# Wide attention on one Trainium2 core: the output projection moved behind the next fills, four exponentials moved ahead of the contexts' copy

## The chip, the cores and the metric

The kernel runs on one core of one Trainium2 chip. The time is device microseconds (us) for one execution of the whole program. Before the change three executions took 1840.51 to 1841.86 us, with a median of 1841.23 us. The core's engines are PE (TensorE; its weight loads are listed as PEld), ACT (ScalarE), DVE (VectorE), POOL (GpSimd) and SP, which issues the loads. Each engine runs its own instructions in order and waits on semaphores for the others.

## The reference

The program is a stack of four gated layers on `x` of shape (32, 128, 128); each has a cross-attention on `ctx` and a feed-forward part. Only the second cross-attention (layer 1, "wide") is touched by the change:

```python
x = x + tanh(g_xattn[1]) * xattn(layernorm(x), ctx, ctx, w_q, w_k, w_v, w_o)
# 32 batches, 128 queries, 128 keys, 16 heads of 64
# q = x w_q^T, k = ctx w_k^T, v = ctx w_v^T       (128 -> 1024 each)
# probs = softmax(q k^T / 8), causal over the 128 x 128 pairs
# out = (probs v) w_o^T                           (1024 -> 128)
```

All of it is in float32; only the causal mask is added in bfloat16.

## The kernel before

The wide attention is the function `attention_wide`. Its unit is a step `n` of 0 to 63: one batch and half of its heads (8 of 16). Every engine has its own loop over `n`, unrolled in the program, and the order of the calls in it is the order on the engine; nothing reorders them. In its iteration `n` PE works on three steps at once: it computes the scores of `n+1`, transposes the probabilities of `n`, and multiplies the contexts of `n-1` with the values.

- `score(n)` writes the causal mask (L1862, four bfloat16 matmuls of 512 columns) and then the products of queries and keys (L1867) into one of two score tiles of two banks each.
- DVE takes the row maxima (`maximum`, L2014). ACT makes the eight exponentials, four per call of `exponents(n, h)`, h = 0 and 1 (L1956). DVE inverts the row sums of each four (`invert`, L2022), POOL multiplies (L1819).
- `turn(n)` (L1907) transposes the probabilities on PE; it waits for both halves from POOL. DVE copies the result back (`copy_turned`, L2007).
- `contexts(n)` (L1883) writes the tile `heads`, a single bank. ACT copies it to `heads_t` (`context_copy`, L1947). `project_out(n)` (L1895) multiplies `heads_t` with `w_o` into `y_ps`. After the second half of a batch DVE adds `y_ps` to `x` (L2028) and takes the statistics (L2033).

Queries, keys and values come in groups of two batches, that is, of four steps. A group has 13 **fills**: x (the normalised input transposed, L1839), k0 to k3 and q0 to q3 (L1848), v0 to v3 (L1842). Each is written by PE (`make`) into one of two banks, `made0` and `made1` in turn, and copied to SBUF by ACT (x, q; L1935, L1938) or DVE (k, v; L2000) in `keep`. So a fill may start only when the fill **two before it** has been copied: `await_kept(pe, f - 2)`. Fills are made one group ahead of their use, at fixed places of the loop (`quarter`): two ahead of `score`, the rest behind `contexts`.

I name the stretches of PE from one mask to the next by what lies in them, in the order in which they follow each other: stretch **Q** (behind its contexts the fill q1, then, for the next iteration, q2 and q3), stretch **V** (v0; v1, v2), stretch **X** (v3; x, k0) and stretch **K** (k1, k2; k3, q0). The semicolon is the border of two iterations; `project_out` stands on it in the kernel before.

```python
                await_kept(pe, f - 2)
                pe.wait_ge(s["heads_done"], n + 1)      # project_out
                wait(act, s["acc_done"], n - 1)         # context_copy
```

Of the kernel before, what the change touches and what calls it, by code (L numbers as in the profile page):

```python
# [24 lines left out]
def wait(eng, sem, value):  # L25

    if isinstance(value, int) and value <= 0:
        return
    eng.wait_ge(sem, value)
# [1712 lines left out]
def attention_wide(nc, st, arg):  # L1742

    layer, PAIR, OCT = 1, 2 * DKW, 2
    NO, CH = NB * OCT, 4
    with ExitStack() as ctx:
# [39 lines left out]
        def place_of(group, kind, part):  # L1786
            return group * NF + order.index((kind, part))

        def fills(n):

            group, part = divmod(n + 4, 4)
            return [group * NF + i for i in quarter[part]] if group < NGR else []

        def await_kept(eng, f):
            if f >= 0:
                own, count = kept_count(f)
                eng.wait_ge(s[own + "_kept"], count)

        def real(n):
            return 0 <= n < NO  # L1800

        def rows(h):
            return slice(h * DKW, (h + 1) * DKW)
# [19 lines left out]
        def _(pe):  # L1823
            pe.wait_ge(st.loads["wide"].sem, st.loads["wide"].total)

            def make(f):
                group, place = divmod(f, NF)
                kind, part = order[place]
                r, out = group % 2, made[f % 2]
                if kind == "x":  # L1830
                    pe.wait_ge(s["xn_done"], group + 1)
                elif (kind, part) == ("k", 0):
                    pe.wait_ge(ctx_in[r], 16 * (group // 2 + 1))
                elif (kind, part) == ("q", 0):
                    await_kept(pe, place_of(group, "x", 0))
                await_kept(pe, f - 2)
                if kind == "x":
                    for u in range(2):
                        last = nc.tensor.transpose(out[:, u * S:(u + 1) * S], xn[:, r, u * D:(u + 1) * D], st.ident[:, :])  # L1839
                elif kind == "v":  # L1840
                    b, half = divmod(part, 2)
                    last = nc.tensor.matmul(out[:, :], ctx_t[:, r, b * S:(b + 1) * S], w_v[:, half * 512:half * 512 + 512],  # L1842
                                            start=True, stop=True)
                else:
                    w, moving = (w_k, ctx_t) if kind == "k" else (w_q, xn_t)
                    for c in range(2):
                        first = (2 * part + c) * PAIR
                        last = nc.tensor.matmul(out[:, c * 2 * S:(c + 1) * 2 * S], w[:, first:first + PAIR], moving[:, r, :],  # L1848
                                                start=True, stop=True)
                last.then_inc(s["made_done"], 1)  # L1850

            def score(n):
                if not real(n):
                    return
                b, o = divmod(n, OCT)
                group, u = divmod(b, 2)
                await_kept(pe, place_of(group, "k", 3))
                await_kept(pe, place_of(group, "q", 3))
                wait(pe, s["pt_done"], 2 * n - 2)
                for h, table in enumerate((st.causal, st.causal_swapped)):  # L1860
                    for r in range(2):
                        nc.tensor.matmul(scores[n % 2][rows((r + h) % 2), h * 512:h * 512 + 512], st.identb[rows(r), rows(r)],  # L1862
                                         table[rows(r), :].unsqueeze(1).to_broadcast([DKW, CH, S]), start=True, stop=False,
                                         skip_group_check=True)
                for c in range(CH):
                    for h in range(2):
                        last = nc.tensor.matmul(scores[n % 2][:, h * 512 + c * S:h * 512 + (c + 1) * S],  # L1867
                                                q_t[rows(h), group % 2, CH * o + c, u * S:(u + 1) * S],
                                                k_t[rows(h), group % 2, CH * o + c, u * S:(u + 1) * S],
                                                start=False, stop=(c == CH - 1), skip_group_check=True)  # L1870
                last.then_inc(s["s_done"], 1)
# [15 lines left out]
            def project_out(n):  # L1887
                if not real(n):
                    return
                b, o = divmod(n, OCT)  # L1890
                pe.wait_ge(s["heads_done"], n + 1)
                if o == 0:
                    wait(pe, s["x_done"], b)
                for c in range(CH):
                    last = nc.tensor.matmul(y_ps[:, 0:D], heads_t[:, n % 2, c * S:(c + 1) * S], w_o[:, CH * o + c, :],  # L1895
                                            start=(o == 0 and c == 0), stop=(o == OCT - 1 and c == CH - 1))
                last.then_inc(s["acc_done"], 1)

            def turn(n):
                if not real(n):  # L1900
                    return
                pe.wait_ge(s["prob_done"], 2 * n + 2)
                for h in range(2):
                    for c in range(CH):
                        for r in range(2):
                            at = r * 512 + (CH * h + c) * DKW
                            last = nc.tensor.transpose(scores[n % 2][:, at:at + DKW], probs[rows(r), n % 2, h, c * S:(c + 1) * S],  # L1907
                                                       st.ident[rows(r), rows(r)])
                last.then_inc(s["t_done"], 2)

            for n in range(-4, NO + 1):
                todo = fills(n)
                for f in todo[:2]:
                    make(f)
                score(n + 1)
                turn(n)
                contexts(n - 1)
                for f in todo[2:]:
                    make(f)
                project_out(n - 1)  # L1920

        @block.scalar
        def _(act):
            ln_scalar(act)

            def keep(f):
                group, place = divmod(f, NF)
                kind, part = order[place]
                if kept_by[place] != "act":
                    return  # L1930
                act.wait_ge(s["made_done"], f + 1)
                if kind == "x":
                    if group >= 2:
                        act.wait_ge(s["made_done"], place_of(group - 2, "q", 3) + 1)
                    last = nc.scalar.activation(xn_t[:, group % 2, :], made[f % 2][:, 0:2 * S], ACT.Copy)  # L1935
                else:
                    wait(act, s["s_done"], 4 * (group - 1))
                    last = nc.scalar.activation(q_t[:, group % 2, 2 * part:2 * part + 2, :].rearrange("p c q -> p (c q)"),  # L1938
                                                made[f % 2][:, :], ACT.Copy, scale=scale)
                last.then_inc(s["act_kept"], 1)  # L1940

            def context_copy(n):
                if not real(n):
                    return
                act.wait_ge(s["pv_done"], n + 1)
                wait(act, s["acc_done"], n - 1)
                nc.scalar.activation(heads_t[:, n % 2, :], heads[:, :], ACT.Copy).then_inc(s["heads_done"], 1)  # L1947

            def exponents(n, h):
                if not real(n):  # L1950
                    return
                act.wait_ge(s["max_done"], n + 1)
                wait(act, s["t_done"], 2 * (n - 2) + h + 1)
                for c in range(CH):
                    i = CH * h + c
                    last = nc.scalar.activation(probs[:, n % 2, h, c * S:(c + 1) * S],  # L1956
                                                scores[n % 2][:, i * S:(i + 1) * S], ACT.Exp,
                                                bias=neg_max[:, n % 2, i:i + 1], accum_out=row_sum[:, n % 2, i:i + 1])
                last.then_inc(s["exp_done"], 1)

            for n in range(-4, NO + 1):
                todo = fills(n)
                for f in todo[:2]:
                    keep(f)
                context_copy(n - 1)
                exponents(n + 1, 0)
                for f in todo[2:]:
                    keep(f)
                exponents(n + 1, 1)
# [308 lines left out]
```

## Time and profile before

| | us |
|---|---|
| median of three executions | 1841.23 |
| profiled execution, its own time | 1840.51 |
| its span | 1838.7 |
| wide attention, from the first mask on PE to the last statistics on DVE | 347.3 to 799 |
| of it one group of four steps, in the steady part | 27.72 |

The span is what the profiler saw from the first to the last instruction; 1.8 us of the execution lie around it. The page lists PE as busy for 92% of the span. In the wide attention every engine's busy time in a group is the same from one group to the next, so one group stands for all of the steady part. In the timeline a fill of queries or keys is four instructions (two matmuls, each in two float32 passes), a fill of values two, a projection eight. A matmul's listed duration holds the time until its result has landed, so that durations overlap; what a piece of work costs PE is read from start to start.

### The profile page before, as it was taken

How to read it: one execution, taken by the hardware profiler on the slowest of the kernel's cores; microseconds unless marked ns; L12 is line 12 of the kernel's file. 1: busy time of each engine (PE TensorE's matmuls, PEld its weight loads, DVE VectorE, ACT ScalarE, POOL GpSimd, SP SyncE). 2: the span in 40 equal slices, each digit the busy share in tenths (PEclk: the TensorE clock that was granted, in tenths of full speed). 3: DMA queues.
4: the chain of work that ended last, by engine and by line, in shares of the span. 5: the costliest groups of instructions: out<-in, count | busy, mean ns of one | idle time of the engine just before them, and what ended most of it. 6: DMA issues, size and time to landing. Idle time of an engine off the chain costs nothing. (4 is left out here: it accounts for less than half of the span.)

```text
span 1838.7 us, 46448 instructions
## 1 busy us (share of the span) xinstructions
PE 1693.0 (92%) x17680; PEld 1105.1 (60%) x17680; DVE 1084.1 (59%) x2348; ACT 870.4 (47%) x2175; POOL 639.9 (35%) x1103
## 2 busy tenths in 40 slices
PE   5999959799999999867988999979999989999798
PEld 2555544577777777665775555546777755555454
DVE  5677657566666666545166676653233236777576
ACT  3555426455655655533544444434343436544354
POOL 4467508322323223300021555510000004676673
PEclk9999959899999999957999999989999989999899
DMA  4000041000000000010101000000000010000000
GB/s 114 2 2 3 2 117 35 9 7 5 8 7 5 7 7 5 2 46 6 41 0 53 2 3 3 3 2 1 1 0 0 0 35 13 2 3 3 1 24 24
DMA packets 47822, 27.64 MB, mean 15 GB/s; under 512 B 11024, under 2 KB 44560, under 8 KB 47632
## 3 DMA queue, kind: packets, MB, share of 16 engines
q1 hardware_dynamic: 42896, 24.64, 4.8%
q8 instruction: 133, 2.18, 0.5%
q10 hardware_dynamic: 4736, 0.35, 0.2%
q14 instruction: 57, 0.47, 0.1%
HBM read 22.88 MB, written 2.10 MB: 14 GB/s over the span
## 5 line engine op out<-in xcount | busy, mean ns | idle before, releaser
L771 DVE TENSOR_REDUCE neg_max<-scores 128x8 f32<-128x1024 f32 x192 | 235.0, 1224 | 134.7 <-PE scores L560 48.9
L1819 POOL TENSOR_TENSOR probs<-probs,inverse 128x512 f32<-128x512 f32 x128 | 133.2, 1041 | 324.6 <-DVE inverse L2022 324.5
L528 PE MATMUL scores<-k_diag,q_all 32*128 32x512 f32 x768 | 216.0, 639 | 0.9 <-DVE dropped L2158 0.9
L542 PE MATMUL turned<-q_diag,k_all 32*128 32x512 f32 x768 | 216.4, 638 | 0.0
L706 ACT ACTIVATE probs<-turned 128x1024 f32<-128x1024 f32 x128 | 131.1, 1024 | 176.5 <-PE turned L574 176.5
L412 POOL TENSOR_TENSOR k_diag<-k_all,hmask 128x512 f32<-128x512 f32 x96 | 100.0, 1043 | 324.2 <-ACT k_all L681 288.4
L1956 ACT ACTIVATE probs<-scores,neg_max 128x128 f32<-128x128 f32 x512 | 180.7, 387 | 5.3 <-DVE neg_max L2014 5.3
L1478 ACT ACTIVATE hidden_f<-hb_f,b_f 128x512 f32<-128x512 f32 x128 | 87.9, 687 | 128.7 <-PE hb_f L1425 128.4
L1434 PEld LDWEIGHTS yb_f<-w_f,hidden_f 128*128 128x128 f32 x1024 | 119.2, 192 | 14.8 <-issue 14.8
L1947 ACT ACTIVATE heads_t<-heads 128x512 f32<-128x512 f32 x64 | 38.2, 597 | 174.5 <-PE heads L1883 174.5
L1434 PE MATMUL yb_f<-w_f,hidden_f 128*128 128x128 f32 x1024 | 119.3, 275 | 0.0
L1956 ACT ACTIVATION_READ_ACCUMULATOR probs<-scores,neg_max 128x1 f32 x512 | 116.7, 228 | 0.0
L1425 PE MATMUL hb_f<-xn_all_f,w_f 128*128 (+1 forms) x256 | 116.5, 599 | 0.0
L1503 DVE TENSOR_TENSOR y_sum_f<-yb_f,b_f 128x512 f32<-128x512 f32 x32 | 22.1, 692 | 150.2 <-PE yb_f L1434 150.2
L418 POOL TENSOR_TENSOR q_diag<-q_all,hmask 128x512 f32<-128x512 f32 x96 | 100.0, 1041 | 30.3 <-PE turned L574 21.3
L608 PEld LDWEIGHTS heads<-probs,ones_pad 128*32 128x32 f32 x3072 | 78.0, 109 | 46.9 <-issue 46.5
L706 ACT ACTIVATE probs<-turned,key_cols 128x1024 f32<-128x1024 f32 x64 | 71.4, 1115 | 70.7 <-PE turned L574 70.7
L597 PE MATMUL heads<-probs,v_pad 128*32 128x128 f32 x3072 | 103.8, 276 | 0.3 <-ACT probs L706 0.2
L608 PE MATMUL heads<-probs,ones_pad 128*32 128x128 f32 x3072 | 103.8, 276 | 0.0
L778 DVE RECIPROCAL inverse<-heads 128x128 f32<-128x128 f32 x96 | 91.0, 948 | 13.8 <-PE heads L608 7.3
L2014 DVE TENSOR_REDUCE neg_max<-scores 128x8 f32<-128x1024 f32 x64 | 78.2, 1222 | 35.3 <-PE scores L1867 35.3
L597 PEld LDWEIGHTS heads<-probs,v_pad 128*32 128x32 f32 x3072 | 78.0, 109 | 33.9 <-issue 31.6
(305 smaller groups left out, 3628.3 us busy)
## 6 DMA issues: line engine op xcount, KB each, us to landing
ctx_t<-in_ctx_t_dram SPq DMA_DIRECT2D x24, 256.0 KB, 2.9
w_f<-in_L_ffn_W_dram SPq DMA_DIRECT2D x16, 256.0 KB, 3.1
x_state<-in_x_dram SPq DMA_DIRECT2D x4, 512.0 KB, 7.6
ctx_t<-in_ctx_t_dram SPq DMA_DIRECT2D x16, 128.0 KB, 2.1
out_dram<-x_state SPq DMA_DIRECT2D x7, 256.0 KB, 2.3
w_f<-in_L_ffn_We_dram SPq DMA_DIRECT2D x1, 1024.0 KB, 7.1
taps_f<-in_L_ffn_conv_w_dram SPq DMA_DIRECT2D x1, 768.0 KB, 6.4
w_e_f<-_ffn_expert_weights_dram SPq DMA_DIRECT2D x1, 512.0 KB, 4.3
```

The source lines that it names most:

```text
L412: p.tensor_tensor(k_diag[:, b % 2, :, :], cols(k_all, b, S).unsqueeze(1).to_broadcast([P, 4, S]), st.hmask4[:, :].unsqueeze(2).to_broadcas ...
L418: p.tensor_tensor(q_diag[:, b % 2, :, :], cols(q_all, b, S).unsqueeze(1).to_broadcast([P, 4, S]), st.hmask4[:, :].unsqueeze(2).to_broadcas ...
L528: last = nc.tensor.matmul(scores[pair][:, (g % 2) * 512:(g % 2 + 1) * 512], cols(q_all, b, S)[quad_rows(g), :], k_diag[quad_rows(g), b % 2 ...
L542: nc.tensor.matmul(turned[:, (g % 2) * 512:(g % 2 + 1) * 512], cols(k_all, b, S)[quad_rows(g), :], q_diag[quad_rows(g), b % 2, :, :].rearr ...
L597: nc.tensor.matmul(heads[b % 2][32 * j:32 * j + 32, 0:S], v_pad[:, b % 2, 128 * g + 32 * j:128 * g + 32 * j + 32], probs[:, b % 2, g // 2, ...
L608: last = nc.tensor.matmul(heads[b % 2][32 * j:32 * j + 32, S:2 * S], ones_pad[:, (3 - g) * DK:(3 - g) * DK + 32], probs[:, b % 2, g // 2, ...
L706: nc.scalar.activation(probs[:, b % 2, pair, :], turned[:, :], ACT.Exp, **bias).then_inc(s["exp_done"], 1)
L771: v.tensor_reduce(neg_max[:, b % 2, 8 * pair:8 * pair + 8], scores[pair][:, :].rearrange("p (h k) -> p h k", k=S), axis=X_AXIS, op=ALU.max ...
L1425: nc.tensor.matmul(hb[c][:, :], w1[:, e, c * P:(c + 1) * P], cols(xn_all, k, BT), start=True, stop=True).then_inc(h_done, 1)
L1434: last = nc.tensor.matmul(yb[e % 2][:, j * D:(j + 1) * D], hidden[:, e % 2, c, j * S:(j + 1) * S], w2[:, e, c, :], start=(c == 0), stop=(c ...
L1819: nc.gpsimd.tensor_tensor(p4, p4, inverse[:, n % 2, CH * h:CH * h + CH].unsqueeze(2).to_broadcast([P, CH, S]), ALU.mult).then_inc(s["prob_ ...
L1956: last = nc.scalar.activation(probs[:, n % 2, h, c * S:(c + 1) * S], scores[n % 2][:, i * S:(i + 1) * S], ACT.Exp, bias=neg_max[:, n % 2, ...
```

## The change

In PE's loop `project_out` goes from the end of the iteration, behind the fills `todo[2:]`, to the place between the fills `todo[:2]` and `score` of the next iteration. In ACT's loop `exponents(n + 1, 0)` goes ahead of `context_copy(n - 1)`. Nothing is computed otherwise, and the number of instructions of every engine is the same.

```diff
-            for n in range(-4, NO + 1):
+            for n in range(-4, NO + 2):
                 todo = fills(n)
                 for f in todo[:2]:
                     make(f)
+                project_out(n - 2)
                 score(n + 1)
                 turn(n)
                 contexts(n - 1)
                 for f in todo[2:]:
                     make(f)
-                project_out(n - 1)
...
                 for f in todo[:2]:
                     keep(f)
+                exponents(n + 1, 0)
                 context_copy(n - 1)
-                exponents(n + 1, 0)
                 for f in todo[2:]:
                     keep(f)
                 exponents(n + 1, 1)
```

PE, stretch X of the kernel before, from the contexts (`heads`) to the next mask (`causal`); `made_1` is the two banks of layer 1, first with v3, then with x and k0:

```order
L1883 MATMUL heads<-probs_t,v_sb 64x128 x8
L1842 MATMUL made_1<-w_v,ctx_t 128x512
L1895 MATMUL y_ps<-w_o,heads_t 128x128 x4
L1839 MATMUL made_1<-ident,xn 128x128 x2
L1848 MATMUL made_1<-ctx_t,w_k 128x256 x2
L1862 MATMUL scores_1<-causal,identb 64x512 x2
```

The same place of the changed kernel:

```order
L1883 MATMUL heads<-probs_t,v_sb 64x128 x8
L1842 MATMUL made_1<-w_v,ctx_t 128x512
L1839 MATMUL made_1<-ident,xn 128x128 x2
L1848 MATMUL made_1<-ctx_t,w_k 128x256 x2
L1895 MATMUL y_ps<-w_o,heads_t 128x128 x4
L1862 MATMUL scores_1<-causal,identb 64x512 x2
```

The projection no longer stands between v3 and the fills x and k0; the three fills follow each other without a break. The same holds for the other three stretches.

ACT beside the stretches K and Q of the kernel before; the first copy to `q_t` is q0, the one between the exponentials q1, the last two q2 and q3:

```order
L1938 ACTIVATE q_t<-made_1 128x512
L1947 ACTIVATE heads_t<-heads 128x512
L1956 ACTIVATE probs,row_sum<-scores_1,neg_max 128x128 x4
L1938 ACTIVATE q_t<-made_1 128x512
L1956 ACTIVATE probs,row_sum<-scores_1,neg_max 128x128 x4
L1938 ACTIVATE q_t<-made_1 128x512 x2
```

The same place of the changed kernel, from the four exponentials on:

```order
L1956 ACTIVATE probs,row_sum<-scores_1,neg_max 128x128 x4
L1947 ACTIVATE heads_t<-heads 128x512
L1938 ACTIVATE q_t<-made_1 128x512
L1956 ACTIVATE probs,row_sum<-scores_1,neg_max 128x128 x4
L1938 ACTIVATE q_t<-made_1 128x512 x2
```

The copy of the contexts now stands between the first four exponentials and q1's copy; q1's copy still has the copy of the contexts and four exponentials ahead of it.

## Rows read from the trace of the kernel before

**Rows 1.** The page: busy time by engine; granted clock of TensorE in 40 slices.

```profile
PE 1693.0 (92%) x17680; PEld 1105.1 (60%) x17680; DVE 1084.1 (59%) x2348; ACT 870.4 (47%) x2175; POOL 639.9 (35%) x1103
...
PEclk9999959899999999957999999989999989999899
```

**Rows 2.** Busy time by stretch, one group: length, engines, granted clock, DMA share, GB/s.

```profile
386.75:414.47 27.72, 27.20 (x283) 20.97 (x282) 17.70 (x36) 15.92 (x73) 8.33 (x8) 1.00 0.02 7
```

**Rows 3.** Waits in 559.77:587.49: total us, times, longest us.

```profile
PEld scores L1907 <- POOL probs L1819: 0.9, 2, 0.5
PE scores L1907 <- POOL probs L1819: 0.5, 2, 0.4
```

**Rows 4.** Timeline of PE, same group: start, us, instruction, [idle before <-releaser].

```profile
559.77 0.40 PE L1862 MATMUL scores<-causal,identb 64*64 64x512 bf16 x2
...
569.72 1.13 PE L1842 MATMUL made<-w_v,ctx_t 128*128 128x512 f32 x2
570.68 1.05 PE L1895 MATMUL y_ps<-w_o,heads_t 128*128 128x128 f32 x8
...
574.62 0.71 PE L1907 MATMUL scores<-ident,probs 64*128 64x64 f32 x16 [0.35 <-POOL probs L1819]
...
576.29 1.99 PE L1848 MATMUL made<-ctx_t,w_k 128*128 128x256 f32 x8
578.12 1.05 PE L1895 MATMUL y_ps<-w_o,heads_t 128*128 128x128 f32 x8
...
583.78 1.13 PE L1848 MATMUL made<-xn_t,w_q 128*128 128x256 f32 x4
...
587.49 0.40 PE L1862 MATMUL scores<-causal,identb 64*64 64x512 bf16 x2
```

**Rows 5.** Timeline, same group: DVE's copy of k1; DVE, ACT and PEld in stretch Q.

```profile
577.46 0.69 DVE L2000 COPY k_t<-made 128x512 f32<-128x512 f32 x1 [0.73 <-PE made L1848]
...
582.38 1.23 DVE L2014 TENSOR_REDUCE neg_max<-scores 128x8 f32<-128x1024 f32 x1 [0.96 <-PE scores L1867]
...
583.89 0.60 ACT L1947 ACTIVATE heads_t<-heads 128x512 f32<-128x512 f32 x1 [2.36 <-PE heads L1883]
584.39 0.36 ACT L1956 ACTIVATE probs<-scores,neg_max 128x128 f32<-128x128 f32 x1
...
585.76 0.62 ACT L1938 ACTIVATE q_t<-made 128x512 f32<-128x512 f32 x1
...
586.43 0.73 PEld L1848 LDWEIGHTS made<-xn_t,w_q 128*128 128x128 f32 x4 [0.17 <-ACT q_t L1938]
```

**Rows 6.** Timeline of the stage's start: fills v3, x, k0, with no projection yet.

```profile
348.74 1.12 PE L1842 MATMUL made<-w_v,ctx_t 128*128 128x512 f32 x2
...
349.71 0.38 PE L1839 MATMUL made<-ident,xn 128*128 128x128 f32 x2
...
350.00 0.68 DVE L2000 COPY v_sb<-made 128x512 f32<-128x512 f32 x1
...
350.80 0.73 PEld L1848 LDWEIGHTS made<-ctx_t,w_k 128*128 128x128 f32 x4 [0.95 <-issue]
...
350.83 1.10 PE L1848 MATMUL made<-ctx_t,w_k 128*128 128x256 f32 x4 [0.74 <-DVE v_sb L2000]
```

**Rows 7.** Timeline of the stage's end, PE, where no fills are left.

```profile
775.30 0.71 PE L1907 MATMUL scores<-ident,probs 64*128 64x64 f32 x16 [1.54 <-POOL probs L1819]
...
777.73 1.16 PE L1895 MATMUL y_ps<-w_o,heads_t 128*128 128x128 f32 x8 [0.70 <-ACT heads_t L1947]
778.82 0.40 PE L1862 MATMUL scores<-causal,identb 64*64 64x512 bf16 x2
...
779.16 1.16 PE L1867 MATMUL scores<-k_t,q_t 64*128 64x128 f32 x16
...
788.42 0.71 PE L1907 MATMUL scores<-ident,probs 64*128 64x64 f32 x16 [2.97 <-POOL probs L1819]
```

**Rows 8.** Busy time by stretch, the stage's last 12 us; columns as in rows 2.

```profile
788.00:800.00 12.00, 8.41 (x64) 7.03 (x64) 2.15 (x5) 1.45 (x3) 0.63 (x9) 0.56 0.00 0
```

## Prediction

> **What bounds the kernel now.** I read the page first: PE is listed as busy for 92% of the span, twice as long as ACT [rows 1], so a change that touches only the order in one stage has to be read from that stage's PE. The busy time by stretch comes next: in one group of the wide attention PE is busy for 27.20 of 27.72 us at a granted clock of 1.00, DVE for 17.70, ACT for 15.92, POOL for 8.33 [rows 2]. The stage is bound by PE's sequence, and what the change can give is what PE waits for. The waits of one group name only one thing of size: PE's transposes wait for POOL's probabilities twice in a group, 0.5 us in PE's own account and 0.9 us in that of its weight loads, which start first [rows 3]; one of the two is seen in the timeline in stretch K [rows 4].
>
> The wait of the projection for ACT's copy of the contexts is not worth anything. From v3 to the projection it is 0.96 us where one fill stands between contexts and projection, and from k1 to the projection 1.83 us where there are two [rows 4]. The second fill is thus 0.87 us; the first has 0.1 us more, which I take for the change from the contexts' half-width weights, as it is there in stretch Q too, where the copy is long done.
>
> **What is removed.** ACT's first four exponentials now wait for the maxima alone. In stretch Q the maxima are done at 582.38 + 1.23 = 583.61, and the first exponential starts at 584.39, behind the copy of the contexts (583.89) [rows 5]. It can start 0.75 us earlier, and so the second four end about as much earlier less what the later places of the copy cost; POOL's second product ends some 0.6 us earlier, more than the longest wait of 0.5 us [rows 3]. All POOL waits of the steady part go: between 0.5 and 0.9 us a group. I take 0.9, the weight loads' account, since PE is idle from where the load could have started.
>
> **What is added.** The projection was PE's cover between fill f and fill f + 2. Start to start a projection takes 0.9 us. Without it three fills follow each other, and the third must wait until the first is copied out of its bank. The path is: a fill's start to DVE's copy 577.46 - 576.29 = 1.17 us, the copy 0.69, and about 0.15 until the matmul starts (350.00 + 0.68 to 350.83) [rows 4 to 6]; together 2.0 us from the first fill's start to the third's.
>
> - Stretch X: v3, x, k0. The fill x is only two transposes. The order that the change makes is in the trace already, once: at the stage's start no projection exists yet, and v3, x, k0 follow each other. PE was idle for 0.74 us before k0, its weight load for 0.95 us, the releaser being the copy of v3 [rows 6]. Bounds 0.74 and 0.95; I take 0.85.
> - Stretches V and K: v0, v1, v2 and k1, k2, k3. Two full fills cover 1.83 us [rows 4] of the 2.0: 0.2 us each, between 0 and 0.3. In K the fill q0 then waits for k2, which is late by no more than k3 is.
> - Stretch Q: q1, q2, q3, with q1 copied by ACT, not DVE. ACT's four exponentials take 585.76 - 584.39 = 1.37 us, the copy of the contexts 0.50 (583.89 to 584.39), the copy of q1 0.62 [rows 5]. From 583.65, where the exponentials now start, this gives 583.65 + 1.37 + 0.50 + 0.62 = 586.14, and a start of q3 at 586.3. Uncovered it could start at 583.78 + 1.83 = 585.6. That is 0.7 us. Before, the same copy ended at 586.38 and q3's load waited 0.17 us for it [rows 5]: the projection was all that hid it. Bounds: 0.4 (if the copy came with no load on ACT in between) and 0.9.
>
> So a group gets 0.85 + 0.2 + 0.2 + 0.7 = 1.95 us of new waits and loses 0.9 us of old ones: +1.05 us. The projection's eight matmuls cost PE the same ahead of a mask as ahead of a fill, within 0.1 us, and the fill that stood ahead of the mask gives the 0.1 back. In the steady part the projection's own wait stays covered: in stretch Q the copy of the contexts ends at 583.65 + 1.37 + 0.60 = 585.6, and the projection, behind q3, starts at 586.3 + 0.9 = 587.2.
>
> The change first acts in the first stretch Q, and acts in 14 groups and one more Q and V: 14 x 1.05 + 0.5 = 15 us. The last X has no x and k0, so no wait.
>
> **The stage's end.** Four iterations have no fills. PE waits 1.54 us for POOL and 0.70 us for the copy in each, and an iteration takes (788.42 - 775.30) / 2 = 6.56 us [rows 7]. With the change its length is set by a new circle: mask 0.34 (778.82 to 779.16), scores and their way to DVE about 1.2, maxima 1.25, four exponentials 1.4, copy of the contexts 0.6, projection 1.1 (777.73 to 778.82) [rows 5, 7], 5.9 us. This gives 0.6 us in each of three iterations and 0.3 us in the first: -2 us. Its last 12 us ran at a granted clock of 0.56, for 8.41 us of PE's work, after PE had been idle for 2.97 us [rows 7, 8]. That idle time shrinks to some 1.7 us. If all ran at the full 2.4 GHz it would be up to 8.41 x 0.44 = 3.7 us less; if nothing changes, 0. I take 1.
>
> **The sum.** The profiled execution took 1840.51 us, a span of 1838.7 and 1.8 around it. 1840.5 + 15 - 2 - 1 = 1852.5. The median is 0.7 us above the profiled execution, so I forecast 1853 us, 12 us or 0.65% slower.
>
> **Rivals.**
>
> *The banks don't bind (faster).* If the copies of the fills came earlier than I have them, as DVE is idle for 0.73 us before k1's copy [rows 5], only the gain would be left: 0.9 us in each of 14.5 groups and 3 us at the end, 1841.2 - 16 = 1825. Against it: DVE is idle there because the fill isn't made yet, not because of its order, so freeing DVE doesn't help; and rows 6 show the wait itself. It decides at the third fill's start: 1.83 us after the first is this case, 2.0 is mine. For X it would need a copy 0.8 us faster. A milder form, in which V, K and Q cost nothing and X alone does, is 14.5 x (0.85 - 0.9) - 3, or 1838.
>
> *The losses and the gains meet (no change).* With the low bounds, 0.74 + 0 + 0 + 0.4 against 0.9, a group costs 0.25 us: +3.6 - 3, or 1842. For it: the bounds. Against: all four have to be low at once.
>
> *The new idle gaps lower the clock (much slower).* Where PE was idle for 2.97 us the clock was at its lower level after it [rows 7, 8]. With gaps of 0.2 to 0.85 us in each stretch it would fall now and then: if one group in ten ran at 1.2 GHz, each up to 27 us longer, 1.5 x 27 = 40 us, or 1890. Against: at the stage's end gaps of 1.54 and 0.70 us stood in an iteration of 6.56 [rows 7], longer gaps than any that I forecast, and the stage's slices on the page stay at 9 [rows 1]. The Trainium skill, "TensorE: Matmul & The Clock Gate", section "A second HAM failure mode: psum-queue depth-cycling", tells of a kernel that went through PSUM banks with frequent small idle gaps and whose clock went up and down for that; by this rule the rival would win, by the rows at the stage's end it loses. The decision goes by the rows.
>
> *The change doesn't do what it says.* The transposes still wait for POOL, because DVE's inversion of the first sums stands behind its copies of the fills and these are later now. Then nothing is gained: 15 + 13 = 28 us in the steady part, 1866. Against: the wait is for the second half, and its inversion comes 0.6 us earlier.
>
> **How the numbers follow.** My forecast with its own range of 1845 to 1862: 0.66. Faster by the banks not binding, with its milder form: 0.13. Meeting within 0.2%: 0.12. The clock: 0.03. POOL still waited for: 0.06. The range is 1840 to 1863: it leaves out the faster cases and the clock. A measurement of this kernel tells 0.2%, or 3.7 us, from no change. Of my forecast 0.03 lies under 1845; so faster 0.13, the same 0.14, slower 0.73.
>
> **What would show it.** In the trace after: the waits of L1907 for POOL gone in the steady part; instead PE or PEld waiting in L1848 for the copy of v3 (about 0.85 us, in each of 14 groups) and for q_t (about 0.7 us, 15 times), and in L1842 and L1848 for copies by about 0.2 us; a group of 28.8 us instead of 27.72 (559.77 to 587.49 [rows 4]); the start of the first exponential right behind the maxima. It is wrong if a group takes less than 27.72 us, if k0 follows x without a wait, or if the granted clock of a group is under 1.00.

## Result: 0.67% slower, and the profile after

| | before | after |
|---|---|---|
| median of six executions, us | 1841.22 | 1853.78 |
| lowest to highest | 1838.88 to 1842.80 | 1846.96 to 1855.04 |
| profiled execution / its span | 1840.51 / 1838.7 | 1854.81 / 1852.7 |
| wide attention, first mask to last statistics | 451.6 | 464.4 |
| one group of four steps | 27.72 | 28.71 |

The ratio is 1.0067, with a 95% interval of 1.0056 to 1.0077. Of the 14.0 us by which the span grew, 12.8 lie in the wide attention; the rest, 1.2 us, lies in stages that the change doesn't touch: 2.75 us more ahead of the stage, 1.5 us less behind it. I didn't follow these up; they may be no more than the difference between two executions.

On the page every engine's busy time is within 5 us of before, and the granted clock of the stage's steady part is 1.00 as before. The busy time by stretch shows it for one group (columns as in [rows 2]):

```profile
562.76:591.47 28.71, 27.65 (x285) 21.27 (x284) 17.77 (x34) 15.92 (x73) 8.33 (x9) 1.00 0.02 6
```

Against [rows 2] the group is 0.99 us longer at the same clock of 1.00, and only 0.45 us of that are listed as PE's busy time. PE's idle time in a group goes from 0.52 to 1.06 us. The waits of PE and its weight loads in this group say for what:

```profile
PEld made L1848 <- ACT q_t L1938: 0.8, 1, 0.8
PEld made L1842 <- DVE v_sb L2000: 0.8, 1, 0.8
PE made L1848 <- DVE v_sb L2000: 0.7, 1, 0.7
...
PE made L1848 <- ACT q_t L1938: 0.4, 1, 0.4
PEld made L1848 <- DVE k_t L2000: 0.3, 1, 0.3
```

The waits of L1907 for POOL [rows 3] are gone, as meant. In their place stand waits of fills (L1842, L1848) for the copy that empties their bank. The 0.8 us of L1842 isn't a loss of that size: PE itself has no wait listed there, and the three fills of stretch V took about 0.2 us more than they would without a wait (below).

The timeline of PE in stretches V and X (mask at 570.05, next masks at 576.86 and 583.73):

```profile
570.05 0.40 PE L1862 MATMUL scores<-causal,identb 64*64 64x512 bf16 x2
...
573.00 3.03 PE L1842 MATMUL made<-w_v,ctx_t 128*128 128x512 f32 x6
...
575.87 1.05 PE L1895 MATMUL y_ps<-w_o,heads_t 128*128 128x128 f32 x8
...
576.86 0.40 PE L1862 MATMUL scores<-causal,identb 64*64 64x512 bf16 x2
...
579.80 1.12 PE L1842 MATMUL made<-w_v,ctx_t 128*128 128x512 f32 x2
...
580.76 0.38 PE L1839 MATMUL made<-ident,xn 128*128 128x128 f32 x2
...
581.80 1.10 PE L1848 MATMUL made<-ctx_t,w_k 128*128 128x256 f32 x4 [0.66 <-DVE v_sb L2000]
...
582.74 1.05 PE L1895 MATMUL y_ps<-w_o,heads_t 128*128 128x128 f32 x8
...
583.73 0.41 PE L1862 MATMUL scores<-causal,identb 64*64 64x512 bf16 x2
```

In stretch X, v3 starts at 579.80 and k0 at 581.80, 2.00 us later, with only x between them. At the same place before, the projection stood between v3 and x [rows 4]. In V the three fills take 2.87 us (573.00 to 575.87). Without a wait they would take 0.96 + 2 x 0.87 = 2.7 us by the pieces of [rows 4], so about 0.2 us is waiting. Stretch Q, on all engines:

```profile
564.30 1.23 DVE L2014 TENSOR_REDUCE neg_max<-scores 128x8 f32<-128x1024 f32 x1 [0.76 <-PE scores L1867]
...
565.56 0.37 ACT L1956 ACTIVATE probs<-scores,neg_max 128x128 f32<-128x128 f32 x1 [2.99 <-DVE neg_max L2014]
565.70 1.59 PEld L1848 LDWEIGHTS made<-xn_t,w_q 128*128 128x128 f32 x8 [0.17 <-issue]
...
566.95 0.61 ACT L1947 ACTIVATE heads_t<-heads 128x512 f32<-128x512 f32 x1
...
567.43 0.62 ACT L1938 ACTIVATE q_t<-made 128x512 f32<-128x512 f32 x1
...
568.10 0.73 PEld L1848 LDWEIGHTS made<-xn_t,w_q 128*128 128x128 f32 x4 [0.81 <-ACT q_t L1938]
568.10 1.13 PE L1848 MATMUL made<-xn_t,w_q 128*128 128x256 f32 x4 [0.40 <-ACT q_t L1938]
```

The first exponential starts 0.03 us after the maxima (564.30 + 1.23), 0.75 us sooner than it did behind the contexts' copy [rows 5]. But q1's copy ends at 568.05, 2.35 us after q1's matmuls began, and q3 starts at 568.10. Two fills cover only 1.8 us of that.

### The profile page after: what moved, and what is told of

It is laid out like the page before. It is cut to its first block and busy times, and to the rows that moved or that the text cites. A ratio compares the mean times of both kernels' runs of the same rounds, so it can differ in the third digit from the quotient of the medians.

```text
span 1852.7 us, 46448 instructions
## 1 busy us (share of the span) xinstructions
PE 1697.3 (92%) x17680; PEld 1108.0 (60%) x17680; DVE 1086.3 (59%) x2348; ACT 870.5 (47%) x2175; POOL 640.0 (35%) x1103
## 2 busy tenths in 40 slices
DMA packets 47822, 27.64 MB, mean 15 GB/s; under 512 B 11024, under 2 KB 44560, under 8 KB 47632
## 5 line engine op out<-in xcount | busy, mean ns | idle before, releaser
L437 POOL CAST spread<-neg_max 128x16 bf16<-128x16 f32 x96 | 24.3, 254 | 192.0 <-issue 166.1
```

## Experiments

Each stretch is read from mask to mask in the steady part of the profile; "stage" is the stage's length in the profiled execution against the 451.6 us of before; the ratio is that of the executions to those of the kernel before that were taken beside them (medians 1840.19 to 1841.22 us). The profile is one execution of each kernel; by how much the clock at the stage's two ends differs in it from kernel to kernel is the subject of the last section.

| kernel | Q | V | X | K | group | stage | median | ratio (95%) |
|---|---|---|---|---|---|---|---|---|
| before | 6.66 | 7.00 | 5.99 | 8.07 | 27.72 | | | |
| after | 7.29 | 6.81 | 6.87 | 7.74 | 28.71 | +12.8 | 1853.78 | 1.0067 (1.0056 to 1.0077) |
| PE part alone | 7.54 | 6.81 | 6.87 | 7.75 | 28.97 | +15.9 | 1855.14 | 1.0085 (1.0071 to 1.0098) |
| ACT part alone | 7.67 | 7.67 | 7.27 | 7.67 | 30.28 | +34.6 | 1876.15 | 1.0187 (1.0174 to 1.0200) |
| after, q1's copy first | 6.80 | 6.80 | 6.87 | 7.74 | 28.21 | +5.3 | 1843.21 | 1.0017 (1.0009 to 1.0026) |
| after, k0 ahead of x | 7.29 | 6.80 | 6.19 | 7.85 | 28.14 | +6.0 | 1845.54 | 1.0022 (1.0011 to 1.0032) |
| after, both | 6.81 | 6.80 | 6.18 | 7.87 | 27.66 | -5.0 | 1837.91 | 0.9979 (0.9970 to 0.9989) |
| late, ACT as before | 6.66 | 7.01 | 5.98 | 8.08 | 27.74 | 0.0 | 1839.57 | 0.9994 (0.9985 to 1.0004) |
| late | 6.62 | 6.77 | 5.98 | 7.81 | 27.18 | -16.0 | 1824.14 | 0.9912 (0.9898 to 0.9925) |
| late, contexts' copy last | 6.62 | 6.62 | 5.98 | 7.50 | 26.71 | -23.0 | 1816.74 | 0.9877 (0.9861 to 0.9894) |

### The two halves of the change, each alone

PE's loop as in the changed kernel, ACT's as before:

```diff
                 for f in todo[:2]:
                     make(f)
+                project_out(n - 2)
                 score(n + 1)
...
-                project_out(n - 1)
```

> The PE part alone: the projection moved behind the next fills, ACT's order as before. My theory (the third fill waits for the first one's copy): the same new waits as in the changed kernel, 0.85 us in stretch X, 0.2 in V and K, and a longer one in Q, because q1's copy now stands behind a later start of the exponentials: 585.76 + 0.62 + 0.15 = 586.5 against 585.6, 0.9 us. The later masks hide POOL without any help from ACT, so no wait for POOL either. A group of 29.0 us, no gain at the stage's end: 1860 us. Rival (the waits for POOL are what ACT's part removes, and without it they stay): a group of 29.9 us or more, 1873 us, and L1907 waiting for POOL in the trace.

ACT's loop as in the changed kernel, PE's as before:

```diff
+                exponents(n + 1, 0)
                 context_copy(n - 1)
-                exponents(n + 1, 0)
```

> The ACT part alone: four exponentials ahead of the contexts' copy, the projection at its old place. My theory: the waits for POOL go (0.9 us a group), but the copy now ends 4.8 us after the mask instead of 3.9, and the projection, 3.9 us after the mask, waits for it: 1.0 us in Q, V and X, 0.1 in K. A group of 29.8 us; 1869 us. The waits for fills stay away. Rival (ACT's part is the whole gain and costs nothing, the loss is PE's part): a group of 26.9 us, 1825 us.

The waits of one group, of PE's part alone:

```profile
PEld made L1848 <- ACT q_t L1938: 1.1, 1, 1.1
...
PE made L1848 <- DVE v_sb L2000: 0.7, 1, 0.7
PE made L1848 <- ACT q_t L1938: 0.7, 1, 0.7
```

and of ACT's part alone:

```profile
PEld y_ps L1895 <- ACT heads_t L1947: 5.0, 4, 1.9
PE y_ps L1895 <- ACT heads_t L1947: 2.6, 3, 1.0
```

PE's part alone has the whole loss of X and a longer Q, and no wait for POOL: later masks hide POOL without any help. The group of 28.97 us is the one that I had worked out; the median of 1855 is 5 us under my 1860. The steady part is 18 us longer, as forecast within 1, but the stage's end is 2 us shorter, where I had put nothing. Its iterations are as long as before (4.90, 6.46 and 6.56 us against 4.89, 6.48 and 6.56). The 2 us lie behind them, where the clock fell as before but came back for the last 4.5 us:

```profile
807.00:810.70 3.70, 3.02 (x32) 2.50 (x32) 1.29 (x2) 0.60 (x1) 0.00 (x0) 0.55 0.00 0
810.70:815.20 4.50, 3.34 (x32) 2.79 (x32) 0.37 (x2) 0.60 (x1) 0.00 (x0) 1.00 0.00 0
```

So they are no effect of PE's part that is shown: the one of the five executions with the lower mean clock, 0.955 instead of 0.960, took my 1860 us.

PE's part alone also tells what ACT's part is worth in the changed kernel. With the waits for POOL gone without it, it gives only the shorter stretch Q, 7.54 to 7.29 us, or 0.26 us a group. ACT's part alone removes the waits for POOL too and pays with the projection's wait for a copy that now comes behind four exponentials. My 29.8 us were short by 0.5, about half of it in X (1.28 us longer than before, where I had put 1.0): there DVE's maxima already start late, behind the normalisation, and with them the four exponentials and the copy. Neither half is a gain alone. Of the rivals, "ACT's part is the whole gain and costs nothing" falls by 51 us.

### The two new waits, each taken away

The changed kernel, on ACT q1's copy ahead of the contexts' copy:

```diff
                 exponents(n + 1, 0)
-                context_copy(n - 1)
                 for f in todo[2:]:
                     keep(f)
+                context_copy(n - 1)
                 exponents(n + 1, 1)
```

> The changed kernel with one change on ACT: q1's copy ahead of the contexts' copy. My theory: q3's wait in stretch Q falls from 0.66 us to about 0.2, since the 0.5 us of the contexts' copy leave its path; the projection has the time to spare. 15 x 0.5 = 7 us less than the changed kernel: 1846 us, a group of 28.2 us, stretch Q 6.8. V, X and K as they are. Rival (Q is long for another reason, the place of the projection ahead of the mask): stretch Q stays at 7.29 us, 1854 us.

The changed kernel, the two fills exchanged:

```diff
-        order = [("x", 0), ("k", 0), ("k", 1), ...
+        order = [("k", 0), ("x", 0), ("k", 1), ...
```

> The changed kernel with the fills x and k0 exchanged, so that k0, a full fill, stands between v3 and the fill that needs v3's bank. My theory: x then waits 0.15 to 0.2 us instead of k0's 0.87; stretch X 6.2 instead of 6.87 us, a group of 28.0, 14 x 0.7 = 10 us less than the changed kernel: 1844 us. Rival (stretch X is long for the three instructions of DVE behind the projection, or for the change from projection to mask): stretch X stays within 0.1 us of 6.87, 1854 us.

Each mend shortens the one stretch that it should and, but for 0.11 us in K, leaves the others: Q from 7.29 to 6.80 us, X from 6.87 to 6.19. With k0 first, PE has no wait for v3's copy in L1848 any more, and the transposes of x start 2.01 us after v3, the same 2.0 us as k0 did, with about 0.2 us of waiting (2.01 us less the 1.83 of two fills) instead of 0.66:

```profile
574.90 1.13 PE L1842 MATMUL made<-w_v,ctx_t 128*128 128x512 f32 x2
575.87 1.03 PE L1848 MATMUL made<-ctx_t,w_k 128*128 128x256 f32 x4
576.91 0.41 PE L1839 MATMUL made<-ident,xn 128*128 128x128 f32 x2
577.15 1.06 PE L1895 MATMUL y_ps<-w_o,heads_t 128*128 128x128 f32 x8
```

So it is the bank, not the place of the projection or the instructions around it. K is longer by 0.11 us. Its transposes start 1.39 us after the mask instead of 1.33, just behind POOL's second product (578.44 + 1.04 = 579.48, transposes at 579.53), and take 0.05 us more. That looks like a small rest of the wait for POOL, which no run tests. The stage's start, before the first stretch Q, is longer by 1.35 us, once. There PE waits 1.73 us for POOL instead of 1.05, ahead of k1, k2 and k3, and the clock is lower behind it. The three fills in the changed kernel, and the same place with k0 first:

```profile
357.80:360.80 3.00, 2.94 (x16) 2.27 (x13) 2.66 (x5) 2.84 (x16) 0.11 (x1) 1.00 0.00 0
```

```profile
355.60:359.90 4.30, 4.30 (x15) 3.51 (x13) 2.66 (x5) 2.23 (x14) 0.59 (x1) 0.62 0.00 0
```

Both mends together (the two diffs above):

> The changed kernel with both mends, q1's copy ahead of the contexts' copy and k0 ahead of x. My theory: the two waits are in different stretches and add up: 28.71 - 0.50 - 0.57 = 27.6 us a group, 16 us less than the changed kernel: 1838 us, and what is left of the loss are the waits of 0.2 us of V, K, X and Q against 0.9 us of POOL. Rival (they share a cause, so that one mend takes most of the other): a group of 28.1 us, 1845 us.

They add up: the groups of the two single mends are 0.50 and 0.57 us under 28.71, which makes 27.64, and 27.66 was measured. The group is then as long as before the change: what is left of the fills' waits eats what POOL's waits gave. In the profile the steady part is 1.0 us shorter than before, the start 1.5 us longer (the clock fell there as it did with k0 first alone) and the end 5.4 us shorter. That profile is of the fastest of 11 executions, so the -5.0 us of its stage are more than the 3.1 us between the medians.

### The projection late, but between the fills

```diff
                 contexts(n - 1)
                 for f in todo[2:]:
                     make(f)
-                project_out(n - 1)
+                project_out(n - 2)
...
-                if n % 2 == 1 and n >= 3:
-                    add_result((n - 3) // 2)
-                    statistics((n - 3) // 2)
+                if n % 2 == 0 and n >= 4:
+                    add_result((n - 4) // 2)
+                    statistics((n - 4) // 2)
```

(PE's and DVE's loops end one iteration later for it.) This with ACT's order of the changed kernel is "late":

> ACT's order as in the changed kernel, the projection a whole step late but at its old place: behind the fills todo[2:] stands project_out(n - 2), whose contexts were copied a step ago; DVE's add and statistics come one iteration later with it. My theory: the projection covers the fills' copies again and waits for nothing, and POOL's results come 0.6 us earlier, so the gain is left without the loss. Waits for POOL fall from 0.9 to about 0.25 us a group: 27.1 us, 9 us less in the steady part, and about 5 us less at the stage's end, where the contexts' copy leaves PE's circle: 1827 us. Rival (the removed waits for POOL are worth nothing since another wait ends at the same time): a group of 27.7, 1837 to 1841 us.

and with ACT's order of before:

> As the kernel before, with the projection a whole step late at its old place (DVE's add with it), and ACT's order as before: the contexts' copy first. My theory: the projection's wait for the copy was worth nothing in the steady part and the waits for POOL stay at 0.9 us: a group of 27.7 us, at the stage's end at most 2 us less: 1840 us. It takes the late projection apart from ACT's order. Rival (the copy's wait of 0.5 us in PEld's account is real time): a group of 27.2 us or less, 1832 us.

The late projection alone moves nothing: 27.74 us, the waits for POOL as in [rows 3]. So the 0.47 us by which the projection's weight load used to wait for the copy were not time. With ACT's new order on top the group falls to 27.18. That is the change's idea without its price, within 0.1 us of what I had worked out. At the stage's end 8 us came instead of 5 (more on that in the last section). What was left in a group of "late":

```profile
PEld scores L1907 <- POOL probs L1819: 0.3, 1, 0.3
```

The last experiment takes that away, by putting the contexts' copy behind all exponentials:

```diff
                 exponents(n + 1, 0)
-                context_copy(n - 1)
                 for f in todo[2:]:
                     keep(f)
                 exponents(n + 1, 1)
+                context_copy(n - 1)
```

> As e5_late, with the contexts' copy behind all eight exponentials on ACT (and q1's copy between the two fours). My theory: what is left of the waits for POOL in e5_late (0.3 us a group in the weight loads' account, in stretch K) is ACT's path of maxima, eight exponentials and the copy of 0.5 us; with the copy off it, it goes. A group of 26.9 us instead of 27.18; 14.5 x 0.3 = 4 us less than e5_late's 1824: 1820 us. The contexts' copy then ends 6.2 us after the mask, still ahead of the next contexts. Rival (the remaining wait is DVE's order): a group of 27.2, 1824 us.

```profile
564.94:591.65 26.71, 26.71 (x283) 21.00 (x282) 17.94 (x34) 15.88 (x74) 8.31 (x9) 1.00 0.03 7
```

PE is now listed as busy for the whole of the group, and waits neither for POOL nor for ACT in it. I had put the group at 26.9 us and the time at 1820; 0.47 us a group came where I had put 0.3, in V and K. At 1816.74 us this kernel is 1.2% faster than the one before the change and, by the two ratios, 1.9% faster than the one after it.

## Why the prediction was right

The forecast was 1853 us with a range of 1840 to 1863; the median is 1853.78. The mechanism is as forecast: a fill waits until its bank has been copied, and that costs more than the waits for POOL gave. That the total agrees to 0.8 us is partly luck: the changed kernel's own executions lie 8 us apart. The terms, one by one:

- **Waits for POOL gone** (0.9 us a group): they are all gone. From mask to contexts V takes 1.93 us instead of 2.31 and K 1.92 instead of 2.50, together 0.96 us less, so this term was right to 0.1. "Late, contexts' copy last", 1.01 us a group under the kernel before, says the same. The reason that I gave, ACT's new order, wasn't needed for it: PE's part alone loses these waits too, since the masks come later. ACT's order pays for most of it only in the late kernels, where no fill waits (27.74 to 27.18 us a group); in the changed kernel it gives 0.26 us, in Q.
- **Stretch X** (+0.85): 6.87 - 5.99 = 0.88. Of it 0.66 is listed as PE's idle time; most of the rest is the tail of x's transposes. The row from the stage's start, where v3, x and k0 once follow each other [rows 6], was the same event as the one in each group. It gave bounds of 0.74 and 0.95, and the 0.85 that I chose between them was 0.03 us off. The lower bound names the copy of v3; the row of the weight load, the upper one, names "issue", not the copy as I wrote.
- **Stretch Q** (+0.7): 7.29 - 6.66 = 0.63. Taking the contexts' copy off the path gave 0.49 back, as its 0.5 us of ACT's time said.
- **V and K** (+0.2 each, against 0.9 of POOL between them): V 0.19 shorter, K 0.33 shorter, together 0.52 against the 0.5 worked out. The fills' share is 0.19 in V and 0.25 in K. The start of the third fill was less exact: its weight load starts 1.91 us after the first fill, between the 1.83 of no wait and my 2.0.
- **Steady part**: from the first mask of Q to the last mask of X it took 416.05 us instead of 401.86: +14.2 against +15.
- **Stage's end**: from that mask to the last statistics 36.62 us instead of 38.05: -1.4 against -3. An iteration takes 5.95 us, as forecast (5.9). Up to the last transposes that gave 2.1 us, as worked out. What failed is the 1 us from the clock, which I had taken to gain from a shorter idle time. The idle time did shrink, from 2.97 to 1.57 us, and yet the last 11 us ran at 0.50, the transposes included, and took 0.7 us more than before.

So two errors, of 0.8 and 1.6 us, that work against each other; the other stages added 1.2. Two slips changed nothing: the chances of "the same" and "slower" add up to 0.15 and 0.72, not 0.14 and 0.73, and of the page's slices only those that lie wholly in the stage read 9, while the one with its end reads 5 [rows 1].

The contexts' rows behind the first term, of V and K, before the change (masks at 559.77 and 572.76):

```profile
562.08 1.09 PE L1883 MATMUL heads<-probs_t,v_sb 128*64 128x128 f32 x16
...
575.26 1.09 PE L1883 MATMUL heads<-probs_t,v_sb 128*64 128x128 f32 x16
```

and after it (masks at 570.05 and 583.73):

```profile
571.98 1.09 PE L1883 MATMUL heads<-probs_t,v_sb 128*64 128x128 f32 x16
...
585.65 1.09 PE L1883 MATMUL heads<-probs_t,v_sb 128*64 128x128 f32 x16
```

Of the rivals, "the banks don't bind" is refuted by the two mends, which gave back 0.50 and 0.57 us a group by taking one wait away each. The clock in the steady part stayed at 1.00 over all of its 416 us, with idle gaps of 0.4 and 0.66 us in every group. The Trainium skill ("TensorE: Matmul & The Clock Gate", "A second HAM failure mode: psum-queue depth-cycling") tells of a bfloat16 kernel with 512 columns that cycled through banks, idled briefly between its matmuls and went up and down in clock. The trace of this float32 kernel, which cycles through two banks and idles twice in a group, shows no such change in the steady part. That POOL would still be waited for is refuted by the waits.

The price wasn't forced by the idea. The order on ACT needs a projection that comes later than the copy; it doesn't need one that leaves the fills without cover. The change moved it by half a step, past two fills; a whole step, to the same place between the fills, keeps the cover.

## What to carry to other kernels

Where one engine fills a small ring of buffers that others empty, an instruction that seems only to sit between two fills may be what hides their emptying. Before moving it, count start to start from a fill to the next one in the same buffer, once with it and once without it, and compare with the path fill, copy, release (here 1.9 to 2.0 us against 1.2 to 1.8). The start or the end of a stage can already show the order that a change will make; here its one wait of 0.74 us gave the price of a wait that then measured 0.66 in each group.

## What the runs showed of the hardware that I had not expected

The granted clock at the end of the stage, where PE waits often, isn't settled by the length of the waits. The changed kernel and the one with both mends have the same instructions, waits and idle times there (1.48 us before each of three projections, 1.57 us before the last transposes). The busy time by stretch of the changed kernel, its last wait and what follows it:

```profile
801.70:803.20 1.50, 0.00 (x0) 0.00 (x0) 0.71 (x3) 0.17 (x2) 1.04 (x1) 0.69 0.00 0
803.20:814.40 11.20, 9.08 (x64) 7.64 (x64) 1.89 (x4) 1.20 (x2) 0.00 (x1) 0.50 0.00 0
```

and of the kernel with both mends:

```profile
784.40:785.90 1.50, 0.00 (x0) 0.00 (x0) 0.71 (x3) 0.18 (x2) 1.03 (x1) 1.00 0.00 0
785.90:793.20 7.30, 5.08 (x64) 4.22 (x64) 1.93 (x4) 1.19 (x2) 0.01 (x1) 1.00 0.00 0
```

From the first to the last of the same 64 matmuls, waits included, it took 11.2 us at 1.2 GHz and about 7.2 at 2.4. In "late" an idle time of 2.5 us, ahead of these matmuls and one more projection, left the clock at its upper level:

```profile
772.60:775.10 2.50, 0.04 (x1) 0.00 (x0) 0.18 (x1) 1.16 (x8) 1.65 (x2) 1.00 0.00 0
775.10:781.70 6.60, 5.83 (x72) 5.11 (x72) 2.58 (x6) 1.19 (x2) 0.00 (x0) 1.00 0.00 0
```

So the length of the last idle time alone doesn't tell whether the clock falls. The mends with k0 first show the other side: 1.7 us of idle time at the stage's start was followed by the lower level, 1.05 us in the changed kernel wasn't. These 4 us are about half of the spread of one kernel's executions, and the time goes with the clock there. With both mends three of 11 executions had a mean clock of 0.959 or 0.960 and took 1833.4 to 1834.0 us; the others had 0.954 to 0.957 and took 1835.4 to 1840.9. The changed kernel took 1846.96 us at 0.961 and 1852.6 to 1855.0 at 0.955 and 0.956. Where in the program those clocks differed wasn't recorded. The clock is also 3.3 of the 5.4 us by which the kernel with both mends is shorter than before at the stage's end in its profile (10.52 to 7.18 us from the last transposes on), and by the same measure, an estimate, about 3 of the 8 us of "late"; fewer and shorter waits account for the rest.
